# Neighbour aggregation ahead of the weight product, with the points on the partitions, in a two-layer point-cloud kernel

## The chip, the cores and the metric

One core of a Trainium2 chip runs the whole program. The metric is the device time of one execution in microseconds. The kernel before took 747.92 us in the median of three runs (745.57 to 748.06).

## What is computed

Inputs: x (2, 512, 1024), a context ctx (2, 1024, 1024) that gives the coordinates of 1024 points in 1024 dimensions for each of two batches, weights fside (2, 512, 512), and the parameters of a small network.

```python
def layer0(ctx, x, fside):
    idx = top_k(-(squared distances of the points of ctx), 8)
    for i in range(4):
        p = where(x >= 0, x, 0.01 * x)
        c = einsum('oi,bin->bon', fside[i % 2], p)                 # one weight per batch of the einsum
        gn = einsum('oi,bikn->bokn', fside[i % 2], p[..., idx])
        x = (c + gn.sum(neighbours)) / 9 + x
    return x
```

In the reference w_center and w_neighbor are the same array fside. Its first axis of length 2 is indexed by the block number 0 to 3, and an index past the end is clamped to the last: block 0 uses fside[0], blocks 1, 2 and 3 use fside[1]. The centre and its eight neighbours are therefore summed with one weight, which is a product with a 0/1 matrix (the adjacency with a one on the diagonal): x += W (p A) / 9.

The second layer takes 30 nearest neighbours in the same distances, builds spherical coordinates from three coordinates of ctx, puts them through three small layers with batch normalization and a softmax over the neighbours, and adds to x the neighbours' columns weighted by it:

```python
    att = softmax(h(ctx[idx30] - ctx), axis=-1)
    out = x + einsum('bnkc,bnk->bnc', x.T[idx30], att)
```

## The kernel before, in words

Every value in float32 that goes through a fast matmul is split in two halves (fp32r high part, low part), so that one exact product takes two or three matmuls.

**Gram stage (build, `first_grams`, `gram`, lines 1389 to 1421).** For each of 16 tiles T (2 batches of 8 tiles with 128 points) TensorE forms the rows of the Gram matrix from about the diagonal on, in the pieces of `PIECES` (line 47), at 8 contraction steps of 3 matmuls (`product`, lines 1385 to 1387). The missing blocks are turned by `turn_blocks` (line 1374) and copied by ScalarE (`mirror_out`), the own ones by `gram_out` (line 600). GpSimd adds the norms of the points (`add_norm`, line 440). For batch 0 the norms come from squares of the staged inputs; for batch 1 as well: ScalarE squares (`square`, line 581), GpSimd adds up (`add_square`, line 448), TensorE averages over partitions (`norms(1)`, line 1353, after gram 11).

**Selection.** VectorE takes the 30 best of each row in 11 steps of maximum, index and replacement (`select_step`, lines 940 to 944), in the order of `FIRST_STEPS` and `STEP_LIST`. After the first three steps of a tile ScalarE writes its adjacency (`adjacency`, line 629), GpSimd adds the diagonal (`diagonal`, line 454), TensorE turns it (`adj_turn`, line 1430), and ScalarE copies it to `nbr` (`nbr_out`, line 620).

**Weights.** TensorE turns both weight matrices (`w_turn`, line 1338, 8 groups of 4), ScalarE and VectorE split them (`w_high`, line 555; `w_low`, line 913). The set that passes 2 to 7 don't use is overwritten after two passes: the first set made, of fside[1], is kept in DRAM and comes back for pass 2.

**Passes.** There are ITS = 8 passes, numbered 0 to 7, alternating between the batches, so that each batch gets its four blocks. State X has channels on the partitions. One pass is 16 steps g:

- eight steps of `wp(g)` (lines 1477 to 1479, 12 matmuls each): y = p W, one point tile each; ScalarE and VectorE split it (`y_high`, line 725; `y_low`, line 978);
- eight steps of `aggregate(g)` (line 1498, 16 matmuls each): y times `nbr`, one channel tile and half of the points each; VectorE updates X (`x_update`, line 986). It waits for y_low of all eight point tiles.

Beside the aggregation stage p for the next pass is prepared, in eight units: ScalarE writes relu(x) and relu(-0.01 x) (`p_halves`, lines 710 and 711), GpSimd joins them (`p_join`, line 483), ScalarE rounds (`p_high`, line 718), GpSimd takes the rest (`p_low`, line 488). Unit n of `p_halves` waits for `p_low` of unit n-2. The next pass's first four `wp` need the first four units, the other four `wp` all eight.

**Side work.** After each step each engine does `side(g)`: selection steps (`SEL_AT`, from `STEPS_AT`), adjacency of batch 1 (`ADJ_AT`), lookups of coordinates (`lookup`, line 1522, two a step from step G0 + 1), and the small network, one item of `NET` a step from M0 on (VectorE mostly; its square roots, arctangent, normalizations and first terms are on ScalarE, in the same queue as `p_halves`). All are written out by hand in the order in which an engine runs them: a wait in one item holds whatever stands behind it.

**The end.** In the last eight steps VectorE makes one-hot factors (`onehots`, lines 1248 and 1257), TensorE spreads the attention weights over a dense matrix (`spread`, line 1582, 16 matmuls), ScalarE copies it (line 834), and X is turned (`turn_x`, line 1597, 4 turns of 128x128 for each of 16 groups) and split (`xT_high`, line 839; `xT_low`, line 1265). Then 16 `attend(i)` (lines 1632 to 1634, 24 matmuls each) with further spreads and turns between them, `result` (line 1304), and a store of 256 KB each.

## Time and profile before

| what | value |
|---|---|
| median of three runs | 747.92 us (745.57 to 748.06) |
| the profiled execution, its own time | 747.99 us |
| its span in the trace | 746.1 us |
| TensorE busy | 720.4 us, 97% |
| VectorE busy | 596.6 us, 80% |
| ScalarE, GpSimd busy | 302.0 us, 258.6 us |
| mean granted clock of TensorE | 0.991 of full |

The span is what the trace covers; the execution's own time is 1.9 us longer. Matmuls are pipelined, so that the durations of neighbours overlap: the distance between starts tells the rate. In the rows, PE is TensorE, DVE VectorE, ACT ScalarE, POOL GpSimd; "idle before" or a number in brackets is the time the engine stood still before the operation, and behind the arrow what ended it.

### The profile page before, as it was taken

The numbers are of one execution on the slowest core, as the hardware profiler recorded it, in microseconds if no ns is written. First come the engines' busy times: TensorE is split into PE (matmuls) and PEld (weight loads), VectorE is DVE, ScalarE is ACT, GpSimd is POOL, SyncE is SP. The second block draws the span as 40 slices with busy tenths as digits, with TensorE's granted clock in tenths as the row PEclk, the third lists the DMA queues.
The fourth block names the chain that finished last, engine by engine and source line by source line (L and its number), as shares of the span: only waits on it lengthen the run. The fifth ranks groups of instructions, "written<-read, shape, count | busy, mean of one in ns | idle before, by whom it ended". The sixth has DMA issues, their size and how long they took to land.

```text
span 746.1 us, 13230 instructions
## 1 busy us (share of the span) xinstructions
PE 720.4 (97%) x5530; PEld 595.1 (80%) x5530; DVE 596.6 (80%) x884; ACT 302.0 (40%) x505; POOL 258.6 (35%) x207
## 2 busy tenths in 40 slices
PE   6999999969999999999999999999998998999998
PEld 4789888858888887888888788888887886777776
DVE  4699999969799999989977979668566777878731
ACT  7436847536634343113302353563552223333210
POOL 2238986955607327203620460651530000000000
PEclk9999999989999999999999999999999999999999
DMA  9612030020002013464300000000000000001001
GB/s 352 215 2 114 1 114 0 1 113 0 1 19 95 2 67 122 164 212 171 125 2 0 1 1 0 1 1 0 1 0 1 2 1 15 30 30 37 36 29 57
DMA packets 21180, 39.88 MB, mean 53 GB/s; under 512 B 10112, under 2 KB 10112, under 8 KB 20864
## 3 DMA queue, kind: packets, MB, share of 16 engines
q1 hardware_dynamic: 20976, 36.93, 14.2%
q10 hardware_dynamic: 144, 2.10, 0.8%
q8 instruction: 44, 0.72, 0.4%
q14 instruction: 16, 0.13, 0.1%
HBM read 32.59 MB, written 6.42 MB: 52 GB/s over the span
## 4 chain that ended last, share of the span: by engine, by line
PE 83%; DVE 8%; POOL 4%; ACT 2%; issue 2%; DMA 1%; SPq 0%; POOLq 0%; DVEq 0%; ACTq 0%
PE bank L1498 31%; PE bank L1477 7%; PE bank L1478 7%; PE bank L1479 7%; PE bank L1522 5%; PE bank L1632 5%; PE bank L1582 4%; PE bank L1633 4%; PE bank L1634 4%; PE bank L1385 2%; PE bank L1387 2%; PE bank L1386 2%; DVE vals L940 2%; DVE idx L942 1%; POOL more L440 1%
## 5 line engine op out<-in xcount | busy, mean ns | idle before, releaser
L1498 PE MATMUL bank<-nbr,pts_l 128*128 128x512 f32 x1024 | 240.9, 393 | 0.4 <-DVE pts_l L978 0.4
L1498 PEld LDWEIGHTS bank<-nbr,pts_l 128*128 128x128 f32 x1024 | 191.7, 189 | 40.5 <-DVE pts_l L978 0.9
L725 ACT CAST pts_l<-bank 128x512 fp32r<-128x512 f32 x64 | 37.6, 588 | 163.5 <-PE bank L1479 163.4
L1477 PE MATMUL bank<-wT,pts_h 128*128 128x512 f32 x256 | 101.2, 395 | 0.0
L1478 PE MATMUL bank<-wT,pts_h 128*128 128x512 f32 x256 | 99.9, 390 | 0.0
L1479 PE MATMUL bank<-wT,pts_h 128*128 128x512 f32 x256 | 99.8, 390 | 0.0
L483 POOL TENSOR_TENSOR scratch<-scratch,q_all 128x512 f32<-128x512 f32 x32 | 43.5, 1365 | 112.1 <-ACT q_all L711 112.1
L986 DVE SCALAR_TENSOR_TENSOR X<-bank,X 128x512 f32<-128x512 f32 x64 | 44.1, 689 | 45.6 <-PE bank L1498 44.5
L834 ACT CAST nbr<-bank 128x512 fp32r<-128x512 f32 x64 | 37.5, 588 | 99.1 <-PE bank L1582 99.1
L1385 PE MATMUL bank<-pts_h 128*128 128x512 f32 (+2 forms) x192 | 70.0, 364 | 7.4 <-DVE pts_l L918 7.4
L488 POOL TENSOR_TENSOR pts_h<-scratch,pts_h 128x512 fp32r<-128x512 f32 x56 | 76.5, 1371 | 0.0
L483 POOL TENSOR_TENSOR scratch<-scratch,more 128x512 f32<-128x512 f32 x24 | 31.4, 1312 | 108.9 <-ACT more L711 108.9
L1387 PE MATMUL bank<-pts_h,pts_l 128*128 128x512 f32 (+2 forms) x192 | 67.4, 351 | 0.0
L1386 PE MATMUL bank<-pts_l,pts_h 128*128 128x512 f32 (+2 forms) x192 | 67.3, 350 | 0.0
L710 ACT ACTIVATE scratch<-X 128x512 f32<-128x512 f32 x56 | 35.3, 631 | 77.9 <-POOL pts_h L488 77.9
L978 DVE TENSOR_TENSOR pts_l<-bank,pts_l 128x512 fp32r<-128x512 f32 x64 | 43.9, 687 | 25.5 <-ACT pts_l L725 24.9
L1479 PEld LDWEIGHTS bank<-wT,pts_h 128*128 128x128 f32 x256 | 48.2, 188 | 10.1
L1477 PEld LDWEIGHTS bank<-wT,pts_h 128*128 128x128 f32 x256 | 48.3, 189 | 9.7
L1478 PEld LDWEIGHTS bank<-wT,pts_h 128*128 128x128 f32 x256 | 48.2, 188 | 9.5
L1582 PEld LDWEIGHTS bank<-scratch 128*128 128x128 bf16 x1024 | 34.3, 98 | 19.4 <-issue 16.8
L1385 PEld LDWEIGHTS bank<-pts_h 128*128 128x128 f32 x192 | 37.0, 193 | 12.2 <-issue 7.3
L1582 PE MATMUL bank<-scratch 128*128 128x64 bf16 x1024 | 41.1, 194 | 3.5 <-issue 3.5
(209 smaller groups left out, 1324.4 us busy)
## 6 DMA issues: line engine op xcount, KB each, us to landing
more<-a_rows SPq DMA_DIRECT2D x17, 480.0 KB, 4.0
scratch<-a_rows SPq DMA_DIRECT2D x15, 480.0 KB, 4.3
X<-in_ctx SPq DMA_DIRECT2D x12, 512.0 KB, 7.0
out_dram<-X SPq DMA_DIRECT2D x16, 256.0 KB, 2.0
more<-in_ctx SPq DMA_DIRECT2D x4, 512.0 KB, 7.0
scratch<-in_fside_BxSxS SPq DMA_DIRECT2D x2, 1024.0 KB, 12.6
w_keep<-wT SPq DMA_DIRECT2D x1, 2048.0 KB, 6.9
X<-in_x SPq DMA_DIRECT2D x2, 1024.0 KB, 6.2
```

Source lines behind the costliest of these rows:

```text
L483: pool.tensor_tensor(p32(n), p32(n), q32(n), ALU.subtract).then_inc(s_p32, 1)
L488: pool.tensor_tensor(p_l[:, t, hf * HALF:(hf + 1) * HALF], p32(n), p_h[:, t, hf * HALF:(hf + 1) * HALF].bitcast(F32), ALU.subtract).then_i ...
L978: dve.tensor_tensor(y_l[:, m, :], bank[g % 3][:], y_h[:, m, :].bitcast(F32), ALU.subtract).then_inc(s_yl, 1)
L986: dve.scalar_tensor_tensor(dst, bank[3 + g % 3][:], 1.0 / (K0 + 1.0), dst, ALU.mult, ALU.add).then_inc(s_xu, 1)
L1385: pe.matmul(o, pts_h[:, k, rows], pts_h[:, k, cols], start=(k == 0), stop=False)
L1386: pe.matmul(o, pts_h[:, k, rows], pts_l[:, k, cols], start=False, stop=False)
L1387: return pe.matmul(o, pts_l[:, k, rows], pts_h[:, k, cols], start=False, stop=(k == KT - 1))
L1477: pe.matmul(bank[g % 3][:], p_h[:, t, cols], wT[:, 0, t, :], start=(t == 0), stop=False)
L1478: pe.matmul(bank[g % 3][:], p_h[:, t, cols], wT[:, 1, t, :], start=False, stop=False)
L1479: mm = pe.matmul(bank[g % 3][:], p_l[:, t, cols], wT[:, 0, t, :], start=False, stop=(t == CT - 1))
L1498: mm = pe.matmul(bank[3 + g % 3][:], y[:, m, t * P:(t + 1) * P], nbr[b][:, m, hf * HALF:(hf + 1) * HALF], start=(m == 0 and part_ == 0), s ...
L1582: mm = pe.matmul(bank[6 + q % 2][:, n * 2 * KP:(n + 1) * 2 * KP], oa[q // 2 % 2][:, m], mv[q // 2 % 2][:, m, 2 * i:2 * i + 2].rearrange("p ...
```

## The change

The state X now has points on the partitions ([P, B, NT, C]); x and fside are handed over with their last two axes exchanged by the host, and so is the output on its way back.

- A pass is first eight steps of `aggregate` (16 matmuls: p times `nbr`, giving q with channels on the partitions), then eight of `wp` (12 matmuls: q times W, updating one point tile of X). The first two units of `aggregate` run together, tile by tile of points. `q_high` and `q_low` take the place of `y_high` and `y_low`, and stand in the aggregation stage; `x_update` stands in the weight stage. p for the next pass is prepared beside the weight stage.
- Weights are loaded as they are needed: no `w_turn`, no copy in DRAM. ScalarE and GpSimd split them from SBUF, the second set from step 32 on, loaded again by a DMA on ScalarE's queue.
- X needs no turns at the end (`turn_x` goes); `xT_high` and `xT_low` read X itself. In `attend` the attention matrix is the stationary operand.
- Norms of batch 1: GpSimd selects the diagonal blocks of the Gram matrix, `norms(1)` sums them, after all Grams.
- Gram rows 3 and 11: columns 384 to 1023 in two pieces of 320, for 256 and 512.
- The selection steps per step, the adjacency of batch 1 and the fourth index rows are placed at other steps; `add_norm` of tiles 14 and 15 goes to step 3.

The diff, cut to its core:

```diff
-    PIECES = [((min(t, 2) * P, HALF, 0), (HALF, N, 1)) if t < 4 else ((min(t, 6) * P, N, 1),) for t in range(NT)]
+    CUTS = (HALF, HALF, HALF, 704)
+    PIECES = [((t * P, CUTS[t], 0), (CUTS[t], N, 1)) if t < 4 else ((min(t, 6) * P, N, 1),) for t in range(NT)]
...
-        p_h, p_l = pts_h[:, 0:CT, :], pts_h[:, CT:2 * CT, :]
+        p_h, p_l = pts_h[:, :, 0:HALF], pts_l[:, :, 0:HALF]
+        q_h, q_l = pts_h[:, :, HALF:N], pts_l[:, :, HALF:N]
...
-        STEPS_AT = (2, 2, 1, 2, 2, 1, 2, 1, 2, 3, 2, 3, 2, 3, 2, 2)
+        STEPS_AT = (2, 3, 2, 3, 2, 3, 2, 2, 2, 2, 1, 2, 2, 1, 2, 1)
...
-        ADJ_AT = {4: (8, 9), 8: (10, 11), 11: (12, 13), 14: (14, 15)}
-        ROWS_AT = {32: 0, 35: 1, 38: 2, 45: 3}
+        ADJ_AT = {3: (8, 9), 6: (10, 11), 8: (12, 13), 12: (14, 15)}
+        W_AT = NT * 4
+        ROWS_AT = {32: 0, 35: 1, 38: 2, 44: 3}
...
+            def w_low(n):
+                t, hi = n % CT, n // CT
+                pool.wait_ge(s_wh, n + 1)
+                pool.tensor_tensor(wT[:, 1 - hi, t, :], w_raw[:, 1 - hi, t, :], wT[:, hi, t, :].bitcast(F32),
+                                   ALU.subtract).then_inc(s_wl, 1)
+
+            def gram_diagonal(T):
+                cols = slice((T - NT) * P, (T - NT + 1) * P)
+                pool.wait_ge(s_gc, pieces_done(T))
+                if T == NT:
+                    pool.wait_ge(s_sqmm, NH)
+                pool.affine_select(out=diag_g[:, cols], in_=score[T][:, cols], compare_op=ALU.is_equal, fill=0.0,
+                                   base=0, pattern=[[-1, P]], channel_multiplier=1).then_inc(s_dg, 1)
...
 # GpSimd, after low_part(7, 1), diagonal(3) and add_norm(5)
+            diagonal(4); p_join(0); p_join(1); add_norm(6); gram_diagonal(8)
+            p_join(2); p_join(3); add_norm(7); gram_diagonal(9); diagonal(5); gram_diagonal(10)
+            p_low(0 to 3); diagonal(6); gram_diagonal(11); p_join(4); p_join(5); p_low(4); p_low(5)
+            gram_diagonal(12); p_join(6); p_join(7); diagonal(7); gram_diagonal(13)
+            p_low(6); gram_diagonal(14); p_low(7); gram_diagonal(15); add_norm(8 to 13)
...
 # ScalarE, after mirror_out(10), gram_out(11) and adjacency(6)
+            p_high(0 to 3); p_halves(4); p_halves(5); mirror_out(11); gram_out(12); nbr_out(5)
+            p_high(4); p_high(5); p_halves(6); p_halves(7); mirror_out(12); gram_out(13); adjacency(7)
+            mirror_out(13); p_high(6); p_high(7); gram_out(14); mirror_out(14); gram_out(15); nbr_out(6); norm_out(1)
...
 # TensorE
             gram(15)
+            adj_turn(6)
+            norms(1)
...
+            def aggregate(g, units=1):
+                it, j = g // (2 * CT), g % (2 * CT)
+                b, hf = it % B, j // CT
+                if it < B and j % CT == 0:
+                    pe.wait_ge(s_nbr, NT * it + NT // 2 * (hf + 1))
+                for u in range(g, g + units):
+                    if u >= 3:
+                        pe.wait_ge(s_ql, u - 2)
...
+                for m in range(NT):
+                    if j == 0:
+                        pe.wait_ge(s_p1, NT * it + m + 1)
+                    for u in range(g, g + units):
+                        t = u % CT
+                        for part_, p in enumerate((p_h, p_l)):
+                            mm = pe.matmul(bank[u % 3][:], p[:, m, t * P:(t + 1) * P],
+                                           nbr[b][:, m, hf * HALF:(hf + 1) * HALF],
+                                           start=(m == 0 and part_ == 0), stop=(m == NT - 1 and part_ == 1))
+
+            def wp(g):
+                it, m = g // NT, g % NT
+                hf, cols = m // CT, slice(m % CT * P, (m % CT + 1) * P)
+                hi = 0 if it < 2 else 1
+                if m % CT == 0:
+                    pe.wait_ge(s_ql, 2 * CT * it + CT * (hf + 1))
...
+                for t in range(CT):
+                    q = hf * CT + t
+                    pe.matmul(bank[3 + g % 3][:], q_h[:, q, cols], wT[:, hi, t, :], start=(t == 0), stop=False)
+                    pe.matmul(bank[3 + g % 3][:], q_h[:, q, cols], wT[:, 1 - hi, t, :], start=False, stop=False)
+                    mm = pe.matmul(bank[3 + g % 3][:], q_l[:, q, cols], wT[:, hi, t, :], start=False,
+                                   stop=(t == CT - 1))
...
             for it in range(ITS):
+                aggregate(2 * CT * it, 2)
+                side(16 * it)
+                side(16 * it + 1)
+                for j in range(2, 2 * CT):
+                    aggregate(2 * CT * it + j)
+                    side(16 * it + j)
                 for m in range(NT):
+                    if 16 * it + NT + m > S0:
+                        spread(2 * (16 * it + NT + m - S0) - 2)
                     wp(NT * it + m)
+                    side(16 * it + NT + m)
...
 # ScalarE, beside wp of pass it
+                for m in range(NT):
+                    if it + 1 < ITS:
+                        n = NT * (it + 1) + m
+                        p_halves(n)
+                        if m:
+                            p_high(n - 1)
+                    side(16 * it + NT + m)
...
+                    lhs = [att_T[c % 2][:, h, r, t] for h in range(2)]
+                    rhs = [a[:, r, :] for a in xT[b]]
```

(The lines for the orders of GpSimd and ScalarE are shortened; calls with "to" stand for one call each.)

## Rows read from the trace of the kernel before

**Rows 1.** The page, its first part: busy time of the engines.
```profile
PE 720.4 (97%) x5530; PEld 595.1 (80%) x5530; DVE 596.6 (80%) x884; ACT 302.0 (40%) x505; POOL 258.6 (35%) x207
```
**Rows 2.** The waits of TensorE: total us, times, longest.
```profile
PE bank L1430 <- POOL scratch L454: 6.3, 1, 6.3
PE bank L1582 <- issue: 3.5, 2, 2.0
PE bank L1374 <- ACT more L600: 1.1, 1, 1.1
```
**Rows 3.** Lines 1477 and 1498 in pass 1: min/median/max ns, first and last start.
```profile
L1477 PE MATMUL bank<-wT,pts_h x32: 389/389/473, 199.3 to 220.5; 128*128 128x512 f32 x32
...
L1498 PE MATMUL bank<-nbr,pts_l x128: 389/389/389, 221.2 to 250.0; 128*128 128x512 f32 x128
```
**Rows 4.** GpSimd's timeline, 222 to 252: start, us, operation, [idle before <- releaser].
```profile
223.10 2.56 POOL L483 TENSOR_TENSOR scratch<-scratch,q_all 128x512 f32<-128x512 f32 x2 [17.09 <-ACT q_all L711]
...
228.23 1.30 POOL L483 TENSOR_TENSOR scratch<-scratch,q_all 128x512 f32<-128x512 f32 x1 [1.32 <-ACT q_all L711]
...
248.88 2.55 POOL L488 TENSOR_TENSOR pts_h<-scratch,pts_h 128x512 fp32r<-128x512 f32 x2
```
**Rows 5.** The chain that ended last, two pieces; TensorE's timeline at 36 us.
```profile
73.27 1.75 PE bank L1338 x16
...
584.03 0.52 PE bank L1597 x4
...
36.18 0.28 PE L1385 MATMUL bank<-pts_h 128*128 128x256 f32 x1
...
36.54 0.28 PE L1385 MATMUL bank<-pts_h 128*128 128x256 f32 x1
```
**Rows 6.** The start: timelines of GpSimd, TensorE; lines 913, 944 and 488.
```profile
148.38 9.35 POOL L440 TENSOR_TENSOR more<-more,X 128x1024 f32<-128x1024 f32 x4
...
L913 DVE TENSOR_TENSOR wT<-bank,wT 128x512 fp32r<-128x512 f32 x8 | 4.9, 676 | 0.0
...
L944 DVE MATCH_REPLACE8 scores<-vals,scores x2: 1207/1207/1207, 128.2 to 129.4; 128x1024 f32<-128x1024 f32 x2
...
167.39 0.84 PE L1498 MATMUL bank<-nbr,pts_l 128*128 128x512 f32 x3
...
L488 POOL TENSOR_TENSOR pts_h<-scratch,pts_h x8: 1276/1292/1306, 174.3 to 204.7; 128x512 fp32r<-128x512 f32 x8
```
**Rows 7.** Preparation after pass 5: timelines of GpSimd and ScalarE; line 488.
```profile
496.51 1.29 POOL L483 TENSOR_TENSOR scratch<-scratch,more 128x512 f32<-128x512 f32 x1 [4.80 <-ACT more L711]
497.76 3.97 POOL L488 TENSOR_TENSOR pts_h<-scratch,pts_h 128x512 fp32r<-128x512 f32 x2
...
491.20 4.19 ACT L751 ACTIVATE scratch<-scratch,stat 128x480 f32<-128x480 f32 x6 [1.61 <-DVE stat L1082]
...
L488 POOL TENSOR_TENSOR pts_h<-scratch,pts_h x8: 1287/1301/2712, 471.1 to 500.4; 128x512 fp32r<-128x512 f32 x8
```
**Rows 8.** Stretches: busy us of PE, PEld, DVE, ACT, POOL, then granted clock; line 1498.
```profile
134.00:136.00 2.00, 1.01 (x9) 1.01 (x10) 1.97 (x5) 1.58 (x5) 2.00 (x2) 1.00 0.00 0
...
580.00:582.00 2.00, 2.00 (x6) 1.61 (x5) 1.27 (x2) 0.00 (x0) 0.00 (x0) 0.50 0.00 0
...
L1498 PE MATMUL bank<-nbr,pts_l x16: 389/512/632, 578.0 to 583.2; 128*128 128x512 f32 x16
```
**Rows 9.** One step of the last pass: VectorE's timeline; a spread in the chain.
```profile
588.81 0.69 DVE L986 SCALAR_TENSOR_TENSOR X<-bank,X 128x512 f32<-128x512 f32 x1 [1.33 <-PE bank L1498]
...
592.02 0.68 DVE L1265 TENSOR_TENSOR pts_h<-bank,pts_h 128x512 fp32r<-128x512 f32 x1
...
588.77 0.48 PE bank L1582 x16
```
**Rows 10.** First and last start of line 1477 in the last pass and of line 1632.
```profile
L1477 PE MATMUL bank<-wT,pts_h x32: 389/389/475, 547.2 to 570.6; 128*128 128x512 f32 x32
...
L1632 PE MATMUL bank<-nbr,pts_h x64: 398/480/775, 617.5 to 687.2; 128*128 128x512 f32 x64
```

More of the change, by code:

```diff
@@ L79, in build @@
         nbr = [nbr0, nbr1]
-        X = sb("X", [P, B, CT, N], F32)
+        X = sb("X", [P, B, NT, C], F32)
+        with nc.sbuf_tensor("w_raw", [P, 2, CT, C], F32) as w_raw:
+            pass
         wT = sb("wT", [P, 2, CT, C], F32R)
@@ L227, in build @@
         s_nbr = sem("nbr_ready")
-        s_x = [sem(f"x_loaded{i}") for i in range(3)]
+        s_dg = sem("gram_diagonal_ready")
+        s_x = [sem(f"x_loaded{i}") for i in range(4)]
         s_p32 = sem("p_ready")
@@ L264, in build @@
         s_scc = sem("spread_copied")
-        s_xT = sem("xT_done")
         s_xTh = sem("xT_high_ready")
@@ L460, in _ @@
             add_norm(1)
+            for n in range(CT):
+                w_low(n)
             add_norm(2)
             diagonal(1)
+            for k in range(4):
+                low_part(k, 0)
             add_norm(3)
-            for k in range(KT):
+            for k in range(4, KT):
                 low_part(k, 0)
@@ L642, in _ @@
             mirror_out(1)
+            for n in range(CT):
+                w_high(n)
             gram_out(2)
@@ L654, in _ @@
             gram_out(4)
-            for n in range(CT):
-                w_high(n)
             mirror_out(4)
@@ L1441, in _ @@
             gram(4)
-            for n in range(CT):
-                w_turn(n)
             gram(5)
@@ L1447, in _ @@
             gram(7)
-            for n in range(CT, 2 * CT):
-                w_turn(n)
             gram(8)
@@ L1456, in _ @@
             gram(11)
-            norms(1)
             adj_turn(5)
@@ L1654 @@
     for name in _INS:
-        a = np.ascontiguousarray(inputs[name])
+        a = np.asarray(inputs[name])
+        a = np.ascontiguousarray(a.transpose(0, 2, 1) if name in ("x", "fside_BxSxS_0") else a)
         arrays[f"in_{name}"] = a
```

441 lines of the change are left out of this document (160 added, 281 removed).

## The prediction

> **What bounds the kernel now.** Read the page's busy line first [rows 1]: TensorE is busy 720.4 of 746.1 us. So this kernel pays for matmul time, and for what keeps TensorE waiting. The waits of TensorE come next [rows 2]: besides the start, where it has no data, 6.3 us at one turn of adjacency blocks held up by GpSimd, 3.5 us in two places near the end, 1.1 us at a Gram turn. Then look at one undisturbed pass [rows 3]: its weight stage (8 units of 12 matmuls) runs from 199.3 to 221.2, 21.9 us, and its aggregation stage (8 units of 16) from 221.2 to 250.2, 29.0 us, with no gap. Last look at what runs underneath [rows 4]: GpSimd and ScalarE prepare p for the next pass, in a chain that starts when ScalarE has finished the stage before. Its eight p_low (L488) end at 251.4, 30.1 us after it could start at 221.3. The period is 3.88 us: a join, a p_low, then 1.32 us in which GpSimd waits for ScalarE.
>
> **TensorE work.** The 1024 aggregation and 768 weight matmuls stay, in number and shape, and so do the attention matmuls; swapping which operand is stationary changes no count. Removed:
> - 32 turns of weights: 16 take 1.75 us [rows 5], so 3.5 us.
> - 64 turns of X: a group of 4 takes 0.52 us beside its neighbours [rows 5], I take 0.5. Eight groups lie in the last pass, eight in the attention part: 4.0 us there.
> - Gram rows 3 and 11: a triple of products takes 0.36 us at 256 columns (distance of starts, [rows 5]) and 0.68 at 512 (three times 21.9 us over 96). Two triples of 320 columns, by interpolation 0.44 each, take the place of 0.36 + 0.68. Eight times 0.16, for two batches: 2.5 us.
> - The two norm matmuls of the second batch are only moved.
>
> The copies of X into halves come from SBUF instead of PSUM, at the same 0.6 us on each engine. On GpSimd seven additions of squares, of the shape of the norm additions (2.34 us each, [rows 6]), become eight selects on a 128x128 diagonal, an eighth of the elements. Between nothing and 2.34 us each, I take 0.4, by the elements; and four weight halves move there from VectorE, 1.3 us each by the p_low of the same shape. Both are in the queue that I follow below. The output and input DMAs carry the same bytes in 2 KB rows; I cost them at nothing, as TensorE's work covers them and only the last store of 256 KB is bare in both.
>
> **The start.** Today six weight units run ahead of the wait for GpSimd, and the wait itself is GpSimd's last norm additions (148.4 to 157.7, [rows 6]). Afterwards nothing may start before the norms of batch 1, which wait for all Gram diagonals and mirrors. I followed each queue by the durations shown. VectorE gives up 8 weight halves (4.9 us in all, [rows 6]), so the eight nearest of tile 7, which it begins to take out at 129.4 today [rows 6], are out near 127, and its adjacency is ready by about 128. Tile 6's is ready near 114. From there GpSimd has four p_low, a diagonal, a select and two joins: 6 times 1.26 and twice 0.4, to 122.9. ScalarE, which waits for the joins, then has a p_high, four halves of p and a mirror copy, 3.5 us, before it copies Gram row 13 out, at 126.6. TensorE, 8 us ahead of today (turns, Gram row, norms, waits), stands at the turn in row 14 from 123.8: a wait of 2.8 us. Row 8 waits 0.7 us for GpSimd's last low part, as its Gram now starts straight behind row 7. Norms end near 133. GpSimd adds the norms of tiles 8 to 13 after that; VectorE stalls some 4 us for the first, but two aggregation units together (7.25 us) cover it. In the first pass the preparation chain also carries adjacency work: now it takes from 167.4 to 206 [rows 6], 38 us, and under the new order it has a weight stage of 21.9 + 1.9 (adjacency turns) and a pair of 7.25, together 31: 6.8 us of waiting, most of it where the turn of tiles 14 and 15 stands behind the chain. With 1.2 us for the clock that makes 11.5 us against 8.6 now (6.3, 1.1, and 1.2 for the clock): +2.9.
>
> **The later passes decide.** Today the chain of 30.1 us has an aggregation stage of 29.0 and half of the next weight stage before its last product is needed. Afterwards it starts with the weight stage, and the first pair needs p of tile m at 21.9 + 0.91 m. Row by row [rows 4], tile 6 is ready at 28.9 and wanted at 27.3, tile 7 at 30.2: a wait of 2.0 us at a plain handover (after pass 1). Handovers after passes 2 and 3 have lookups in the weight stage and wait for nothing. After passes 4, 5 and 6 the network's work on ScalarE stands in the chain. The case after pass 5 shows today as a join 4.80 us late, behind six normalizations of 4.19 us in all [rows 7]. These come sooner after the change, since the stage under them is faster, so I take 2.1 us of delay, a wait of 4.5 us in all; 4.0 after pass 6, 2.5 after pass 4. Sum 13.0. After an idle of 2.05 us the granted clock stood at 0.50, the 1.2 GHz level, and one unit took from 578.0 to 583.4, 5.4 us for 3.6 to 3.8 [rows 8]; after the idle of 1.1 us it stayed at 1.00. That is 1.6 us for each long wait, two of them: 3.2. Together +16.2.
>
> **The end.** In the last pass VectorE must make one-hots (two spreads a step), update X and take xT_low: 3.82 us a step, from 588.81 to the end of L1265's share [rows 9]. The step was 5.2 us long; it becomes 2.74 + two spreads of 0.48 = 3.70, so VectorE just becomes the bound. The first spread waits 6.1 us after the stage before ends, over a unit of 2.75. I get 36.4 us, and 31.1 us for the aggregation stage ahead of it, for the present 70.3 (547.2 to 617.5 [rows 10]): -2.8 rather than the -4 of the turns alone.
>
> **Sum**, on the profiled execution (span 746.1, time 747.99, 1.9 around it; the median of the runs is 747.92, the same): -3.5 - 2.5 + 2.9 + 16.2 - 2.8 - 4.0 = +6.3. Span 752.4, time 754.
>
> **Unknowns and bounds.** The wait per later handover lies between 0 (a chain that overlaps better than the rows) and the full delay seen today (33 and 35 us chains, waits of 4 to 6.7): 0 to 18 us in all, against my 13. The start lies between no wait at all (-11) and 8 us more than mine. Clock: 0 to 6.
>
> A page speaks on the handover too. The row: one p_low took 2712 ns for 1301 in the median, while VectorE worked on the network [rows 7]. The Trainium skill, page "SBUF — State Buffer", section "SBUF: two separate sides", says that a VectorE operation with two SBUF inputs and a GpSimd one share a port pair as an exclusive lock, held for the whole instruction. By that rule each network step that meets the chain would block it; today there was slack for that, afterwards there is none.
>
> **Rivals.**
> 1. *The pair hides the chain* (faster). Place: the handovers after passes 1, 4, 5, 6. If p is ready within 29.2 us of the stage's end, the 16.2 goes away and 738 us is left. For: the pair doubles the time over the eight tiles. Against: 3.88 us a tile, measured eight times. With only the plain 2.0 us at each of four, and no clock cost, 746, no change.
> 2. *The start goes worse* (slower than mine). Norms of the second batch come so late that VectorE's selection, then the halves of q, then the third unit wait: 8 us more, 762.
> 3. *The shared port.* One p_low stretched by 1.4 us at each of three network handovers: 4 us more, 758.
> 4. *The change doesn't do what it says*: that aggregation ahead of weights leaves less work. It doesn't, by count; only the turns go.
>
> **Chances.** My case (waits of 9 to 18 us) 0.45, 749 to 761; plain waits only 0.22, 742 to 750; hidden 0.20, 735 to 743; start worse 0.07; port 0.06. A change of 0.5% (744.2 to 751.7) is about what a measurement of this kernel can tell from none. Faster by more: the hidden case and a third of the plain one, 0.27. Same: the rest of that and a fifth of mine, 0.24. Slower: 0.49. The range, 740 to 762, leaves out the better part of the hidden case and little else; my case alone would be 749 to 761.
>
> **What would show it.** Right: TensorE waits for GpSimd's p_low at the first unit of passes 2, 5, 6 and 7, 2 to 5 us each, with a lower granted clock behind the long ones; a wait at Gram row 14; weight stages still 21.9 us; last-pass steps near 3.8. Wrong: no wait on p_low over 1 us, or p_low's period other than 3.9 us; or the largest wait at the norms, which would move the cause to the start.

## The result, and the profile after

The changed kernel took 770.93 us in the median (768.94 to 772.31) and the kernel before, on the same chip, 747.89. The ratio is 1.031, with a 95% interval of 1.028 to 1.035. The forecast was 754 us with a range of 740 to 762: the sign is right, the size is wrong, and the time lies above the range. The profiled execution took 771.61 us, its span is 769.8 against 746.1, so 23.7 us are to be explained where 6.3 were forecast.

The page of the changed kernel, busy time of the engines and the granted clock in 40 slices:
```profile
PE 725.2 (94%) x5434; PEld 595.1 (77%) x5434; DVE 589.1 (77%) x876; ACT 294.8 (38%) x497; POOL 253.0 (33%) x216
...
PEclk9999999999999998989999999998998998999999
```
TensorE has 96 instructions fewer than before and yet shows 4.8 us more of busy time than in [rows 1]. That is a first sign of the clock: a matmul at half clock counts as busy for longer. The mean granted clock fell from 0.991 to 0.965.

TensorE's waits in the changed kernel: total us, times, longest. They answer to [rows 2]:
```profile
PE bank L1440 <- POOL pts_l L490: 11.9, 7, 2.6
...
PE bank L1487 <- issue: 4.7, 11, 0.8
PE bank L1545 <- DVE scratch L1247: 3.4, 1, 3.4
PE bank L1392 <- POOL scratch L445: 3.4, 2, 2.9
PE bank L1487 <- ACT a_row L721: 3.2, 1, 3.2
PE bank L1340 <- ACT more L605: 2.7, 1, 2.7
```
L1440 is the aggregation and L490 is p_low: these are the waits at the handovers, where the first two aggregation units of a pass (the pair) need the p that was prepared under the weight stage before. L1340 and L1392 are the start. L1487 is the lookup, in passes 2 and 3, and no term of my sum stood for it. Where the list says "issue", the profile names nothing that ended the wait.

To see where the time came from, cut both traces at the same points of the program: the end of pass 1, of pass 3, then pass by pass, and the attention part last. Columns: stretch, length, busy time of PE, PEld, DVE, ACT and POOL, granted clock, DMA share, GB/s. First the kernel before:
```profile
0.00:250.19 250.19, 235.06 (x1252) 198.58 (x1253) 219.41 (x299) 138.06 (x217) 148.54 (x125) 0.99 0.22 77
250.19:393.37 143.18, 141.09 (x1893) 119.69 (x1892) 131.82 (x220) 36.77 (x68) 45.97 (x33) 1.00 0.33 113
393.37:444.89 51.52, 51.07 (x226) 41.96 (x224) 43.34 (x46) 22.38 (x36) 19.90 (x15) 1.00 0.00 1
444.89:495.94 51.05, 51.05 (x227) 42.27 (x226) 37.51 (x66) 25.50 (x44) 17.89 (x15) 1.00 0.00 1
495.94:547.23 51.29, 51.29 (x229) 42.43 (x228) 35.36 (x77) 23.57 (x43) 22.55 (x17) 1.00 0.00 1
547.23:617.50 70.27, 66.83 (x525) 55.39 (x523) 50.31 (x82) 23.32 (x43) 3.78 (x5) 0.98 0.00 1
617.50:746.10 128.60, 123.98 (x1184) 94.77 (x1184) 78.88 (x96) 32.38 (x56) 0.00 (x0) 0.99 0.09 34
```
Then the changed kernel, the same stretches:
```profile
0.00:246.91 246.91, 232.36 (x1221) 196.17 (x1221) 212.97 (x291) 125.77 (x199) 133.97 (x125) 0.99 0.17 56
246.91:407.54 160.63, 149.84 (x1894) 124.82 (x1893) 134.58 (x224) 42.23 (x79) 55.77 (x41) 0.94 0.32 107
407.54:458.31 50.77, 50.77 (x226) 42.05 (x224) 39.99 (x44) 18.32 (x29) 14.55 (x11) 1.00 0.00 0
458.31:514.03 55.72, 53.40 (x228) 43.12 (x226) 36.33 (x65) 25.47 (x45) 20.33 (x17) 0.97 0.00 1
514.03:572.06 58.03, 54.08 (x229) 43.95 (x228) 36.05 (x75) 24.18 (x44) 20.36 (x16) 0.94 0.00 1
572.06:646.43 74.37, 65.92 (x494) 52.88 (x492) 50.30 (x87) 26.54 (x48) 8.04 (x8) 0.93 0.00 1
646.43:769.80 123.37, 118.82 (x1152) 92.16 (x1152) 78.90 (x96) 32.31 (x56) 0.00 (x0) 0.97 0.10 35
```
Subtract the lengths, and set beside them what the prediction's terms give for each stretch (its 3.2 us for the clock put with the handovers after passes 5 and 6):

| stretch | after minus before | forecast |
|---|---|---|
| start to the end of pass 1 | -3.3 | -3.5 - 2.5 + 2.9 = -3.1 |
| passes 2 and 3 | +17.5 | +2.0 (handover after pass 1) |
| pass 4 | -0.8 | 0 |
| pass 5 | +4.7 | +2.5 |
| pass 6 | +6.7 | +4.5 + 1.6 |
| pass 7 | +4.1 | +4.0 + 1.6 - 2.8 = +2.8 |
| attention part | -5.2 | -4.0 |
| sum | +23.7 | +6.3 |

So 15.5 of the missing 17.4 us lie in passes 2 and 3, and 4.1 more in passes 5 to 7, where the granted clock is 0.97 to 0.93 and was 1.00 to 0.98 before; the start, pass 4 and the attention part differ from the forecast by 0.2, 0.8 and 1.2 us, in the kernel's favour.

The handovers look as forecast. After pass 1, GpSimd's p_low in the changed kernel, and who waited for it (us, times):
```profile
L490 POOL TENSOR_TENSOR pts_l<-scratch,pts_h x8: 1271/1300/1313, 229.6 to 254.1; 128x512 fp32r<-128x512 f32 x8
...
  ACT scratch L701: 13.0, 6
  PEld bank L1440: 2.5, 2
  PE bank L1440: 1.6, 1
```
The last p_low ends at 255.35, 30.2 us after the weight stage began at 225.15, and the chain of [rows 4] had 30.1. The line `ACT scratch L701: 13.0, 6` points at the cause of the period: ScalarE waits six times, 13 us together, for a p_low to give a buffer back.

What I had not looked for is in passes 2 and 3. VectorE beside the lookups in the weight stage of pass 3 (367.65 to 392 us) of the changed kernel, then in the aggregation stage ahead of it (316.02 to 366), where GpSimd is busy for 0.38 us in all. L993 makes the one-hots of a lookup, L999 compares the low bits of the indices; the numbers behind the bar are busy us and the mean ns of one:
```profile
L993 DVE TENSOR_SCALAR more<-more,part 128x1920 bf16<-128x1920 bf16 x4 | 6.2, 1569 | 0.0
L999 DVE TENSOR_TENSOR scratch<-scratch,iota_r 128x120 bf16<-128x120 bf16 x8 | 5.6, 698 | 0.1
L993 DVE TENSOR_SCALAR scratch<-scratch,part 128x1920 bf16<-128x1920 bf16 x3 | 2.4, 817 | 0.0
```
```profile
L993 DVE TENSOR_SCALAR more<-more,part 128x1920 bf16<-128x1920 bf16 x8 | 5.4, 712 | 0.0
L999 DVE TENSOR_TENSOR scratch<-scratch,iota_r 128x120 bf16<-128x120 bf16 x16 | 4.5, 280 | 0.3
```
The same instruction takes 712 ns in one stage and 817 to 1569 in the next, 280 against 698. What differs is that GpSimd prepares p there. Before the change that preparation lay under the aggregation stages, where a step of TensorE with two lookups is long; now it lies under the weight stages, where it is short. This became the main theory for the experiments.

### The profile page after: what moved, and what is told of

Read it like the earlier page. It is cut to its first block, busy times and chain, and to the rows that moved or that the text cites. A ratio compares the mean times of both kernels' runs of the same rounds, so it can differ in the third digit from the quotient of the medians.

```text
span 769.8 us, 13026 instructions
## 1 busy us (share of the span) xinstructions
PE 725.2 (94%) x5434; PEld 595.1 (77%) x5434; DVE 589.1 (77%) x876; ACT 294.8 (38%) x497; POOL 253.0 (33%) x216
## 4 chain that ended last, share of the span: by engine, by line
PE 61%; POOL 15%; ACT 11%; DVE 9%; issue 3%; DMA 1%; ACTq 0%; SPq 0%; DVEq 0%; POOLq 0%
PE bank L1440 23%; POOL scratch L485 7%; POOL pts_l L490 7%; PE bank L1487 5%; PE bank L1578 4%; PE bank L1545 4%; PE bank L1580 4%; PE bank L1579 4%; ACT scratch L701 3%; PE bank L1351 3%; PE bank L1353 3%; PE bank L1352 3%; PE bank L1462 2%; PE bank L1463 2%; PE bank L1464 2%
## 5 line engine op out<-in xcount | busy, mean ns | idle before, releaser
L1440 PE MATMUL bank<-nbr,pts_h 128*128 128x512 f32 x512 | 208.5, 407 | 12.0 <-POOL pts_l L490 11.9
L1440 PE MATMUL bank<-nbr,pts_l 128*128 128x512 f32 x512 | 205.1, 401 | 0.0
L1440 PEld LDWEIGHTS bank<-nbr,pts_h 128*128 128x128 f32 x512 | 99.8, 195 | 37.9 <-POOL pts_l L490 16.3
L1440 PEld LDWEIGHTS bank<-nbr,pts_l 128*128 128x128 f32 x512 | 99.8, 195 | 20.7 <-issue 0.2
L1462 PE MATMUL bank<-wT,pts_h 128*128 128x512 f32 x256 | 104.5, 408 | 0.0
L1463 PE MATMUL bank<-wT,pts_h 128*128 128x512 f32 x256 | 102.1, 399 | 0.0
L1464 PE MATMUL bank<-wT,pts_l 128*128 128x512 f32 x256 | 101.7, 397 | 0.0
L1351 PE MATMUL bank<-pts_h 128*128 128x512 f32 (+3 forms) x192 | 69.9, 364 | 7.5 <-DVE pts_l L913 7.1
L490 POOL TENSOR_TENSOR pts_l<-scratch,pts_h 128x512 fp32r<-128x512 f32 x56 | 75.1, 1346 | 0.0
L1352 PE MATMUL bank<-pts_l,pts_h 128*128 128x512 f32 (+3 forms) x192 | 67.3, 351 | 0.0
L1353 PE MATMUL bank<-pts_h,pts_l 128*128 128x512 f32 (+3 forms) x192 | 67.2, 350 | 0.0
L701 ACT ACTIVATE scratch<-X 128x512 f32<-128x512 f32 x56 | 35.3, 631 | 83.1 <-POOL pts_l L490 83.1
L1464 PEld LDWEIGHTS bank<-wT,pts_l 128*128 128x128 f32 x256 | 49.5, 193 | 10.9
L1578 PE MATMUL bank<-pts_h,nbr 128*128 128x512 f32 x128 | 55.5, 434 | 0.8 <-ACT nbr L827 0.8
```

The lines of the kernel that those rows point to most:

```text
L490: pool.tensor_tensor(p_l[:, m, :], p32(n), p_h[:, m, :].bitcast(F32), ALU.subtract).then_inc(s_p1, 1)
L701: act.activation(p32(n), src, ACT.Relu).then_inc(s_pr, 1)
L1351: pe.matmul(o, pts_h[:, k, rows], pts_h[:, k, cols], start=(k == 0), stop=False)
L1352: pe.matmul(o, pts_h[:, k, rows], pts_l[:, k, cols], start=False, stop=False)
L1353: return pe.matmul(o, pts_l[:, k, rows], pts_h[:, k, cols], start=False, stop=(k == KT - 1))
L1440: mm = pe.matmul(bank[u % 3][:], p[:, m, t * P:(t + 1) * P], nbr[b][:, m, hf * HALF:(hf + 1) * HALF], start=(m == 0 and part_ == 0), stop= ...
```

## The experiments

All times are medians; the ratio is against the kernel before, run on the same chip in the same session, and is taken over the runs: it is not the quotient of two medians and differs from it by up to 0.25% (run 8). The changed kernel stands at 1.0313 on this scale. What an edit is worth is given below by the difference of ratios, in us of 748. The kernel before scatters between 745.2 and 748.7 us, and its median was 745.59, 747.38, 747.66 and 747.58 in the four sessions of the table, so a difference of 0.3% between rows of different sessions tells little. Stage lengths come from one profiled execution of each kernel.

| run | edit | us | ratio (95%) |
|---|---|---|---|
| 1 | p in place | 745.8 | 0.9998 (0.998 to 1.001) |
| 2 | waits filled | 760.95 | 1.0199 (1.018 to 1.022) |
| 3 | index row first | 768.63 | 1.0306 (1.028 to 1.033) |
| 4 | no chain beside the lookups | 756.29 | 1.0147 (1.013 to 1.017) |
| 5 | one unit first | 783.85 | 1.0503 (1.048 to 1.052) |
| 6 | one unit first, p in place | 747.95 | 1.0019 (1.001 to 1.003) |
| 7 | kernel before, p in place | 753.34 | 1.0097 (1.007 to 1.012) |
| 8 | p in place, row first, lookups dealt by stage | 736.25 | 0.9876 (0.986 to 0.990) |
| 9 | lookups dealt by stage alone | 767.43 | 1.0247 (1.021 to 1.029) |
| 10 | kernel before, lookups dealt by stage | 756.42 | 1.0116 (1.010 to 1.014) |
| 11 | p in place, row first | 743.8 | 0.9949 (0.993 to 0.996) |
| 12 | run 8, spreads one step ahead | 729.89 | 0.978 (0.976 to 0.980) |

**Run 1, p in place.** The same operations, with p in the slot that its low half will take, and the small buffers only for the negative part, which the join frees:
```diff
         def p32(n):
...
-            return scratch[:, 11 * U + (n % 2) * HALF:11 * U + (n % 2 + 1) * HALF]
+            return q_all[:, n % NT, 0:HALF]
         def q32(n):
...
-            return more[:, 3, (n % 2) * HALF:(n % 2 + 1) * HALF]
+            return scratch[:, 11 * U + (n % 2) * HALF:11 * U + (n % 2 + 1) * HALF]
...
-                if n >= 2 * CT:
-                    act.wait_ge(s_p1, n - 1)
+                if n >= NT:
+                    act.wait_ge(s_p32, n - 1)
+                    if n < NT + 2:
+                        act.wait_ge(s_p1, n - 1)
...
```


> The changed kernel with p kept in its own slot of the low half (eight slots in place of two buffers), so that ScalarE no longer waits for the p_low of two tiles before. Chain theory: GpSimd's period falls from 3.88 us to its two operations, 2.6, tile 7 is ready some 24 us after the stage before, ahead of the pair; the handover waits (1.8, 2.3, 4.05 and 3.4 us after passes 1, 4, 5 and 6) and the clock losses behind them (8.3 us) go, about -20 us, 751 us. Rival, shared port: the same GpSimd operations packed denser stretch VectorE more, and half of it is given back in the lookups: 760. Rival, the waits were for the operations and not for the buffer: period stays near 3.9, no change, 771.

Measured: 745.8 us, 24 us less than the changed kernel. GpSimd's timeline after pass 1, from the first join to the last p_low; no idle time stands in brackets any more behind the first row:
```profile
219.40 2.55 POOL L483 TENSOR_TENSOR q_all<-q_all,scratch 128x512 f32<-128x512 f32 x2 [25.59 <-ACT scratch L700]
221.91 1.31 POOL L488 TENSOR_TENSOR pts_l<-q_all,pts_h 128x512 fp32r<-128x512 f32 x1
223.17 1.30 POOL L483 TENSOR_TENSOR q_all<-q_all,scratch 128x512 f32<-128x512 f32 x1
...
237.00 2.56 POOL L488 TENSOR_TENSOR pts_l<-q_all,pts_h 128x512 fp32r<-128x512 f32 x2
```
The period is 2.52 us, the chain ends 22.1 us after the stage began (217.48), and TensorE's waits for p_low are gone from its list. It was the buffer that set the period. The gain is larger than I wrote down: passes 0 and 1, where the same chain held up TensorE, are shorter too, by 6.7 us (from 133.23 to 225.15 in the changed kernel, from 132.31 to 217.48 here), which I had not counted. The lookups go the other way:
```profile
356.08:400.21 44.13, 38.07 (x553) 31.72 (x550) 38.67 (x56) 11.88 (x22) 21.92 (x16) 0.88 0.18 58
```
This is the weight stage of pass 3. It took 39.9 us in the changed kernel (367.65 to 407.54) and takes 44.1 here: the denser chain costs the lookups 4 us.

**Run 2, waits filled.** Matmuls whose result nobody reads, 51 in all by the table `FILL_AT`, stand in front of the waits:
```diff
                     if j == 0:
+                        for n in range(FILL_AT.get((it, m), 0)):
+                            if n == 0:
+                                pe.wait_ge(s_xu, NT * it - 2)
+                            pe.matmul(bank[3 + NT * it % 3][:], p_h[:, 0, 0:P], nbr[b][:, 0, 0:HALF],
+                                      start=True, stop=True)
                         pe.wait_ge(s_p1, NT * it + m + 1)
```


> The changed kernel with matmuls whose result is never read put in front of the waits at the first pair of passes 2, 5, 6 and 7 (8, 10, 18 and 15 of 0.23 us, by the measured waits). Nothing is computed sooner. Theory that idle time of TensorE lowers the granted clock: the low stretches behind these waits (3.4, 3.4, 6.8, 6.8 us) go and 8.3 us come back: 763. Rival, the clock falls with other things than idle time: 771 to 772.

Measured: 760.95 us, 1.1% or 8.5 us faster than the changed kernel, by work that computes nothing. The first stretch of passes 2, 5, 6 and 7, changed kernel:
```profile
246.91:257.50 10.59, 8.91 (x35) 6.62 (x34) 4.92 (x10) 4.11 (x8) 6.31 (x5) 0.90 0.00 0
458.31:469.50 11.19, 9.04 (x34) 6.81 (x33) 5.49 (x6) 4.71 (x10) 6.29 (x6) 0.89 0.01 1
514.03:528.00 13.97, 10.02 (x35) 7.51 (x34) 6.19 (x7) 7.54 (x14) 6.92 (x5) 0.77 0.00 0
572.06:586.00 13.94, 10.69 (x36) 8.05 (x35) 6.74 (x16) 7.69 (x12) 7.70 (x6) 0.77 0.00 0
```
and with the waits filled:
```profile
247.16:257.50 10.34, 10.24 (x45) 7.98 (x44) 5.09 (x10) 4.57 (x10) 6.34 (x5) 1.00 0.00 0
458.52:469.00 10.48, 10.29 (x45) 8.06 (x44) 5.24 (x5) 4.72 (x10) 6.38 (x6) 1.00 0.01 2
512.91:526.00 13.09, 12.90 (x55) 9.91 (x54) 6.16 (x7) 7.68 (x14) 7.02 (x5) 1.00 0.01 1
569.18:582.00 12.82, 12.64 (x54) 9.69 (x53) 6.14 (x14) 7.60 (x12) 7.76 (x6) 1.00 0.00 1
```
Length times the missing share of the clock is 1.1 + 1.2 + 3.2 + 3.2 = 8.7 us in the first four rows and nothing in the others. So it is TensorE's idle time that lowers the clock here, and that costs some 8.5 us beside the waits of 11.9, where I had allowed 3.2. The place is less sure than the sum: in the two profiled executions the four aggregation stages with the waits took 134.8 us for 140.5, 5.7 less, and another 2.95 came in the last weight stage and the attention part (157.15 for 160.10), where the edit does nothing. Why these two parts of the gain split in this way is not shown.

**Run 3, index row first.** On ScalarE, L721 ahead of the p halves of its step:
```diff
-                if g in TURN_AT:
+                if g in TURN_AT and g % 16 < NT:
                     a_row_out(TURN_AT[g])
...
                         n = NT * (it + 1) + m
+                        if 16 * it + NT + m in TURN_AT:
+                            a_row_out(TURN_AT[16 * it + NT + m])
                         p_halves(n)
```


> The changed kernel with ScalarE's last copy of a turned index row (L721) put ahead of the p halves of its step instead of behind them. Queue theory: the first lookup no longer waits 3.25 us, and the half clock behind it (1.9 us lost) goes: 766. Rival, VectorE's one-hots are the bound of the whole stretch of lookups: what starts sooner waits later, 769 to 771.

Measured: 768.63 us. By the ratios that is 0.07% under the changed kernel, less than the intervals tell; the time itself is 2.3 us lower and lies between the two forecasts. In the changed kernel ScalarE's row is
```profile
298.65 0.63 ACT L701 ACTIVATE scratch<-X 128x512 f32<-128x512 f32 x1 [2.62 <-POOL pts_l L490]
...
300.22 0.25 ACT L721 CAST a_row<-bank 128x128 bf16<-128x128 f32 x1
```
so a copy of 0.25 us stood behind a wait for GpSimd. With it out of the way the 3.2 us are gone from the list, while lookups wait for their one-hots 1.9 us where it was 0.8:
```profile
PE bank L1489 <- DVE more L995: 1.9, 2, 1.1
```
The three stages that carry lookups (the weight stage of pass 2 and all of pass 3), first in the changed kernel, then in this run:
```profile
280.67:407.54 126.87, 118.07 (x1764) 99.82 (x1764) 106.70 (x177) 32.09 (x59) 44.29 (x32) 0.93 0.38 127
```
```profile
280.31:403.76 123.45, 117.44 (x1763) 99.34 (x1763) 106.53 (x177) 32.18 (x59) 44.03 (x32) 0.96 0.39 130
```
They are 3.4 us shorter, 2.8 of it idle time of TensorE (length less busy time, 6.01 for 8.80), so in this pair of executions little of the wait came back elsewhere. Whether the edit alone gains 0 or 3 us stays open between the ratios and the traces. On top of p in place the same edit is worth 0.5% by the ratios, 3.7 us, and 2.0 us by the medians (run 11 against run 1).

**Run 4, no chain beside the lookups.** The 16 joins and 16 low parts under the two weight stages with lookups work on 16 columns; ScalarE's work stays, with the negative part written over the positive one:
```diff
+            if 24 <= n < 40:
+                return p32(n)
...
-                pool.tensor_tensor(p32(n), p32(n), q32(n), ALU.subtract).then_inc(s_p32, 1)
+                w = P // 8 if 24 <= n < 40 else HALF
+                pool.tensor_tensor(p32(n)[:, 0:w], p32(n)[:, 0:w], q32(n)[:, 0:w], ALU.subtract).then_inc(s_p32, 1)
...
```


> The changed kernel in which GpSimd's joins and low parts of p for passes 3 and 4 (16 of each, under the weight stages that carry lookups) work on 16 columns of 512; that part of p is left out of the result. Shared port theory: VectorE's one-hots in the weight stage of pass 3 fall from 1.57 and 0.82 us to 0.71 and L999 from 0.65 to 0.28; the lookups' waits in passes 2 and 3 (11.1 us) and the clock lost there (5.2) go: 755. Rival, a weight stage with two lookups a step is too short for VectorE's own work: only the 3.25 us wait and its clock go, 765.

Measured: 756.29 us, by the ratios 12 us less than the changed kernel. VectorE in the weight stage of pass 3 (361.47 to 385), and the whole of that stage:
```profile
L1006 DVE TENSOR_TENSOR scratch<-scratch,iota_r 128x120 bf16<-128x120 bf16 x10 | 2.8, 284 | 0.2
L1000 DVE TENSOR_SCALAR scratch<-scratch,part 128x1920 bf16<-128x1920 bf16 x3 | 2.1, 713 | 0.0
```
```profile
361.47:395.47 34.00, 34.00 (x553) 29.03 (x549) 28.36 (x56) 12.60 (x22) 4.44 (x15) 1.00 0.25 75
```
The one-hots are at 713 ns and the comparisons at 284, and TensorE is busy for all of the 34.00 us of the last stage, 5.9 us shorter than in the changed kernel. So a weight stage with two lookups a step is long enough for VectorE by itself, which the rival denied, and too short only beside GpSimd. The three stages with lookups:
```profile
280.82:395.47 114.65, 113.11 (x1764) 96.62 (x1763) 92.08 (x177) 33.57 (x59) 8.28 (x32) 0.99 0.44 140
```
They take 12.2 us less than in the changed kernel: 7.3 us of idle time (1.54 for 8.80) and 5.0 us of busy time, which goes with the clock, 0.99 for 0.93. Not all of it is VectorE's: without the chain the index row's copy isn't late either, and run 3, which moves that copy alone, has 3.4 of the 12.2. The 8.8 us between run 3 and this run are what the chain costs beside that. The list of waits wouldn't have told: 3.7 us of the lookups' waits in the weight stage of pass 3 stand there as "issue", and 0.3 us are left of all such waits here.

By the Trainium skill, page "SBUF — State Buffer", section "SBUF: two separate sides", GpSimd shares a port pair with VectorE operations in a fast two-port mode or with two SBUF inputs. The trace agrees in which operations stretch (those on bf16 in SBUF) and which don't: the multiplication that reads a bank kept its 0.53 us in both stages. The Trainium skill's page speaks of a lock for the whole instruction. In the changed kernel the longest one-hot took 1.75 us for 0.71 and the longest comparison 1.37 for 0.28: 1.0 and 1.1 us more, a little less than the 1.3 us of one GpSimd operation, so the lengths don't speak against it. That it is a port, and no other thing the two engines share, is the Trainium skill's word; the runs show only that VectorE's operations stretch while GpSimd works.

**Runs 5 and 6, one unit first.** The pair (the first two aggregation units run together) undone, on the changed kernel and on run 1:
```diff
-                aggregate(2 * CT * it, 2)
+                aggregate(2 * CT * it)
                 side(16 * it)
+                aggregate(2 * CT * it + 1)
                 side(16 * it + 1)
```


> The changed kernel with its first two aggregation units one after the other again. Chain theory: the first unit then wants tile 7 3.2 us after the stage before and not 6.4, so each handover that waits for p waits some 3.5 us longer (after passes 0, 1, 4, 5, 6), and the low clock grows by one stretch at some: 17 to 22 us more than the changed kernel, 788 to 792. Rival, most of the wait is elsewhere (ScalarE's side work) and the pair hides little: 770 to 775.

> The same undo on top of p kept in place (745.8 us with the pair). Chain theory: tile 7 is ready some 24 us after the stage before and wanted at 25: the pair is worth nothing after passes 1 to 4 and 1 to 3 us after passes 5 and 6, 746 to 752. Rival, the pair is needed whatever the chain's period: over 757.

Measured: 783.85 and 747.95 us. The pair saves 1.9%, 14 us, beside the slow chain, where I had expected 17 to 22: without it the waits for p_low are 23.7 us and not 11.9. Beside the quick chain it saves 0.2%. The pair is a cover for the chain, as the prediction read it, and hides little else.

**Runs 7 and 10, the same edits on the kernel before.**

> The kernel before with p kept in place, the same edit as in the first run. Theory that its chain was hidden by the order weights, aggregation: no handover waited, so nothing comes back, within 0.3% of before; at most the waits of its lookups (2.1 us in pass 3) move by 1 to 2 us either way, since GpSimd's operations beside VectorE's one-hots are denser. Rival, a shorter period helps wherever it stands: over 1% faster.

> The kernel before with its lookups dealt out in the same way, 3 to an aggregation step and 1 to a weight step. There GpSimd's chain lies under the aggregation stage, so this puts more of VectorE's lookup work beside it. Theory of the shared port: three one-hots and picks a step, stretched, take some 8.5 us for a step of 7.2; in 6 such steps of pass 3 up to 8 us are lost and at most 2.8 us of waits are won: 747 to 754. Rival, dealing by the length of the stage helps in either order: 743 to 745.

Measured: 1.0097 and 1.0116. Both make the kernel before slower. In run 7 a quicker chain brings nothing, as expected, since it was hidden; but it lies under the aggregation stage with the lookups of pass 3, and there the loss is 1%, more than the 0.3% I wrote. That stage took 45.8 us before (347.60 to 393.37) and takes 51.0 here (348.32 to 399.35), with the clock at 0.93 for 1.00, and VectorE's comparisons there take 929 ns in the mean for 780. Dealing three lookups to the steps beside GpSimd costs 9 us, 2 more than the worst that I had written, in the direction of the same theory; its waits were not taken apart further. Run 7 is the price of a denser GpSimd beside VectorE in the other order of stages.

**Runs 8, 9 and 11, lookups dealt by stage.** Three to an aggregation step, one to a weight step, so that most of them meet an idle GpSimd. VectorE picks one lookup later, and its first picks stand ahead of the one-hots of the same step (not shown):
```diff
+        def looked(g):
+            return sum(3 if q % 16 < NT else 1 for q in range(G0 + 1, min(g, G0 + TILES) + 1))
...
-                for u in (2 * (g - G0) - 2, 2 * (g - G0) - 1):
-                    if 0 <= u < 2 * TILES:
-                        lookup(u)
+                for u in range(looked(g - 1), looked(g)):
+                    lookup(u)
...
```


> p in place, the index row's copy first, and the 32 lookups dealt out 3 to an aggregation step and 1 to a weight step in place of 2 and 2, with VectorE's picks one lookup later. Theory that the lookups lost time because VectorE's step beside GpSimd (6.4 us) is longer than a weight step with two lookups (5.1): waits of 14 us and 6.7 us of half clock in passes 2 and 3 go, new ones of 1 to 4 us come since VectorE has 6.9 of 7.2 us in an aggregation step: 726 to 732. Rival, VectorE is the bound of the stretch however it is dealt out: 740 to 746.

> The changed kernel with only the lookups dealt out 3 to an aggregation step and 1 to a weight step; p and the index row's copy as in the change. If the losses at the handovers and those of the lookups are separate terms: the handovers keep their 11.5 us and 8.3 of clock, the lookups' stretch gives back what it gave on top of p in place (9.5 us) and up to 3 more, less the 3.2 us wait for the index row, which stays: 757 to 762. Rival, the two are one loss (the slow chain makes the lookups late): under 3 us, over 766.

> p in place and the index row's copy first, lookups still 2 and 2: what lies between the run with p in place (745.8) and the one with the lookups dealt by stage (736.3). If the gain there came from the dealing: 744 to 746. Rival, it came from the row's copy, which there stands ahead of a quicker chain: 736 to 740.

Measured: 736.25, 767.43 and 743.8 us. By the ratios dealing is worth 0.7% both times: run 9 against the changed kernel (1.0313 to 1.0247, 5 us) and run 8 against run 11 (0.9949 to 0.9876, 5.5 us). By the medians it is 3.5 and 7.5 us, so whether it gives as much beside the slow chain isn't settled. It is about half of what I wrote for runs 8 and 9. Run 9's time, 767.43, lies in the range of its rival, "over 766"; its gain, 3.5 to 5 us, lies above the rival's "under 3". The trace speaks for two terms: in run 9 the three stages took 122.90 us for 126.87, while the waits for p_low stayed at 12.0 for 11.9 and so did the wait for the index row, 3.2. In run 8 the three stages take 116.5 us (271.28 to 387.78), near the 114.65 of run 4. The profiled execution was the quickest of the five, though, 732.17 us with a clock of 0.990 where the others have 0.981 to 0.984. The weight stage of pass 3 has no wait at all, and what is left in the aggregation stage is one wait of 2.2 us for a one-hot and a clock of 0.94:
```profile
359.45:387.78 28.33, 28.33 (x328) 23.36 (x325) 26.15 (x37) 10.98 (x20) 20.48 (x15) 1.00 0.03 10
```

**Run 12, spreads one step ahead.** The last wait over 3 us behind the start:
```diff
-                if T0 + 2 <= g < T0 + 2 + CHUNKS:
-                    round_high(g - T0 - 2)
+                for c in {T0 + 2: (0,), T0 + 3: (1, 2), T0 + 4: (3,)}.get(g, ()):
+                    round_high(c)
...
-                if T0 + 3 <= g < T0 + 3 + CHUNKS:
-                    att_parts(g - T0 - 3)
-                if g >= S0:
-                    onehots(g - S0)
+                for c in {T0 + 3: (0,), T0 + 4: (1, 2), T0 + 5: (3,)}.get(g, ()):
+                    att_parts(c)
+                if g == S0 - 1:
+                    onehots(0)
+                if g > S0:
+                    onehots(g - S0)
```


> The kernel with p in place, the row's copy first and the lookups dealt by stage (736.3), and VectorE's parts of the attention weights and its first one-hots for the spreads one step sooner. Theory that the last pass's first spread waits for VectorE alone: the wait of 3.6 us and the 1.6 us of half clock behind it go, 731. Rival, the q_low that VectorE now does later hold up the weight stage instead: 735 to 737.

Measured: 729.89 us, ratio 0.978. The wait for the spread's one-hots, 3.4 us in run 8, is gone from TensorE's list. The gain over run 8 is 1.0%, 7 us, where I had written 5. In the profiled executions the last weight stage and the attention part took 153.3 us for 157.2, and the rest of the gain wasn't traced. The kernel beats the one before by 2.2% and the changed one by 5.2%. The page's busy line:
```profile
PE 703.6 (97%) x5434; PEld 582.0 (80%) x5434; DVE 583.7 (80%) x876; ACT 293.7 (40%) x497; POOL 251.2 (35%) x216
```
With as many instructions as the changed kernel (13026), TensorE is busy 21.6 us less, with a mean clock of 0.991 for 0.965: for the most part matmuls that ran at half clock.

## Why the prediction was wrong, step by step

Two steps failed. The prediction put the cost of the chain beside the lookups at nothing, and the runs show 12.2 us in the three stages that carry them. And its term for the clock at the handovers was 3.2 us, where run 2 gave back 8.5.

- **TensorE's work and the start: right in the sum, not in its parts.** Turns -3.5, Gram rows -2.5, waits +2.9 gave -3.1; the trace shows -3.3 at the end of pass 1. The wait at Gram row 14 is 2.69 us at 125.56 (2.8 forecast), and norms end at 133.2 (near 133). The diagonal selects take 0.29 us each, I took 0.4. The waits for GpSimd's adjacency work in the first pass (L1392) are 3.4 us, with another 0.9 at the first unit of pass 1, against 6.8 forecast for that handover: some 2.5 us better. The clock was misread on both sides, at 1.2 us each. Before, it stood at 0.57 from 155 to 163 us, behind the wait of 6.3: 3.4 us. In the changed kernel it stood at 0.52 from 125.56 to 129.10 and at 0.63 from 186 to 190.5: 3.4 us again. Waits and clock of the start come to 10.9 us after the change (2.7 + 0.5 + 3.4 + 0.9 + 3.4) and 10.8 before (6.3 + 1.1 + 3.4): +0.1 where I had +2.9. That the end of pass 1 came out as forecast is thus luck: with +0.1 it would be -5.9 for the -3.3 measured, so 2.6 us went elsewhere ahead of it, which was not traced.
- **Waits at later handovers: right in size.** Forecast after passes 1, 4, 5 and 6: 2.0, 2.5, 4.5 and 4.0, 13.0 together; measured 1.6, 2.1, 4.0 and 3.3, 11.0 together. Run 1 shows that they come from the chain and its buffer, runs 5 and 6 how much of it the pair covers.
- **The clock: mis-sized.** "1.6 us for each long wait, two of them: 3.2." The rows of run 2 have 8.7 us of missing clock behind these four waits, and run 2 gave back 8.5 in all. I priced one low stretch by one unit of [rows 8] and said that only the long waits would be followed by one. In the changed kernel's profile all four were, and those after passes 5 and 6 by a loss of 3.2 us each.
- **Passes 2 and 3: the step that failed.** "Handovers after passes 2 and 3 have lookups in the weight stage and wait for nothing." That holds for the handovers (run 4 and the changed kernel have no wait for p_low there), but I looked only at who waits for the chain, and not at who works beside it. Moving the chain from the aggregation stages to the weight stages put it beside VectorE's lookups where a step of TensorE is shortest. The three stages from the weights of pass 2 lose 12.2 us by it (126.87 against 114.65 in run 4), as waits and as the lower clock behind them. Of these 3.4 us go with the 3.2 us wait for the index row's copy, queued behind the chain on ScalarE (123.45 in run 3), a wait that the sum also lacked; 8.8 go with the chain beside VectorE.
- **Rival 3 named the mechanism and missed the place.** I priced the shared port at 4 us, at the network's handovers, with a chance of 0.06. I had taken from the Trainium skill's rule its half on operations with two inputs in SBUF; the one-hots, with one tensor input, stretched as well, which fits its half on the fast two-port mode. The port's real place was in view: before the change the one-hots took 711 ns in the weight stage of pass 3 (307 to 347 us) and 1314 in the aggregation stage behind it, in lines that I had not read:
```profile
L1003 DVE TENSOR_SCALAR scratch<-scratch,part 128x1920 bf16<-128x1920 bf16 x8 | 5.5, 711 | 0.0
```
```profile
L1003 DVE TENSOR_SCALAR scratch<-scratch,part 128x1920 bf16<-128x1920 bf16 x4 | 5.2, 1314 | 0.0
```
- **Last pass and attention: near, but for the handover.** The weight stage with the spreads took 36.7 us (36.4 forecast). The aggregation stage took 37.6: 31.1 forecast, and the rest is its handover and the clock. The attention part gave 5.2 us, I had 4.0.
- **Rivals 1 and 2** fell: the pair didn't hide the chain, and the start wasn't worse. What rival 4 says of the count holds: TensorE has 96 instructions fewer, the 32 and 64 turns.

The sum with these terms, +6.3, 12.2 for the lookups and 5.3 more for the clock, is +23.8 against 23.7. The agreement to 0.1 us is luck. Passes 2 and 3 are 15.5 us over the forecast, and 12.2 with 1.1 of clock at their handover make 13.3: 2.2 us there have no term. Against them stand handover waits 2 us lower than forecast, pass 4 with 0.8 and the attention part with 1.2 us less.

## What to carry to other kernels

When a chain of side work (here ScalarE and GpSimd preparing p) moves from one stage to another, ask two questions and not one: who waits for it there, and which engine works beside it there. Compare the duration of the same instruction over stages, with the other engines idle and busy; a mean over the kernel hides it. And before a chain is covered with a wider first unit, see whether its period is work or a buffer given back late: here it was the buffer, 1.32 of 3.88 us.

An edit's worth goes with the order of the stages around it: p in place gave 3% in one order and took 1% in the other.

## What the runs showed of the hardware

- VectorE's bf16 operations in SBUF (one-hots, 128x1920, 711 ns; comparisons, 128x120, 280 ns) took in the mean 1.2 to 2.2 and 2.5 times as long beside GpSimd's subtractions in the changed kernel. The multiplication that reads a bank kept its 532 ns, and so did the reduction with a single f32 input in SBUF (L1006, 528 ns in both stages). With the denser chain of run 1 the comparison's mean rose to 1198 ns.
- The same idle time can cost the clock or not. After pass 1, TensorE waited 1.65 us in the changed kernel and had a mean clock of 0.88 to 258 us; in run 3, with the same instructions up to there and a wait of 1.7 us, it had 1.00:
```profile
246.91:258.00 11.09, 9.41 (x36) 7.02 (x35) 5.42 (x12) 4.59 (x9) 6.31 (x5) 0.88 0.02 1
```
```profile
247.06:258.00 10.94, 9.24 (x40) 6.98 (x39) 5.72 (x12) 4.78 (x10) 6.31 (x5) 1.00 0.04 6
```
  A wait near 2 us is thus a chance of a loss and not a fixed price. What decides it in a given execution is left open.
